# Silu on ScalarE in one instruction, in place of a tanh there and a product on VectorE

## The reference

```python
xz = xn @ W_in
xb, z = jnp.split(xz, 2, axis=-1)                 # 512 channels each
xp = jnp.pad(xb, ((0, 0), (1, 1), (0, 0)))
xb = conv_w[:, 0] * xp[:, :-2] + conv_w[:, 1] * xp[:, 1:-1] + conv_w[:, 2] * xp[:, 2:] + conv_b
xb = jax.nn.silu(xb)
dt = jax.nn.softplus(xb @ W_dt + b_dt)
Bi, Ci = xb @ W_B, xb @ W_C
# 16 states per channel, over the tokens:
#   h = exp(dt * A) * h + (dt * x) * B ;  y = sum over states of h * C
y = (y + D_param * xb) * jax.nn.silu(z)
return residual + y @ W_out
```

## Time and profile before

| | |
|---|---|
| median of 3 runs | 2777.06 us (2775.08 to 2786.98) |
| profiled execution | span 2779.7 us; its own time is told by this span alone |
| granted TensorE clock, mean | 0.941 |
| busy | PE 86%, DVE 87%, POOL 80%, ACT 56% of the span |
| table loads | 64 before L921, 49 before L1028 |

### The profile page before, as it was taken

How to read it: one execution, slowest core, us unless ns; L and a number is a source line. 1 busy time by engine, 2 the same in 40 slices (tenths; PEclk the granted TensorE clock), 3 DMA queues, 4 the chain that set the end, 5 groups by cost and what they waited for, 6 DMA issues and landing times.

```text
span 2779.7 us, 29004 instructions
## 1 busy us (share of the span) xinstructions
PE 2379.4 (86%) x9004; PEld 1687.3 (61%) x9004; DVE 2424.8 (87%) x2450; ACT 1565.3 (56%) x2961; POOL 2234.5 (80%) x1563
## 2 busy tenths in 40 slices
PE   3445798998989899898989999898999989898899
PEld 1222466666756666675666667666666756666678
DVE  2688999999999999999999999999999999999922
ACT  3556666566566656655665655566565556665311
POOL 1578888888888888888898888888888888987922
PEclk8677899999999899999999999999999999999999
DMA  4689898999989899998989989898998989898921
GB/s 113 172 209 231 220 236 219 229 237 218 239 221 235 218 227 235 222 236 214 234 224 238 232 220 244 213 233 218 241 231 218 241 205 235 222 245 210 241 64 50
DMA packets 338380, 596.80 MB, mean 215 GB/s; under 512 B 49696, under 2 KB 160288, under 8 KB 338224
## 3 DMA queue, kind: packets, MB, share of 16 engines
q0 software_dynamic: 72960, 243.30, 45.6%
q1 hardware_dynamic: 265264, 351.64, 40.3%
HBM read 349.89 MB, written 10.06 MB: 129 GB/s over the span
## 4 chain that ended last, share of the span: by engine, by line
PE 25%; POOL 22%; issue 17%; DVE 17%; ACT 10%; DMA 8%; SPq 0%; POOLq 0%; DVEq 0%; ACTq 0%
POOL unit L1199 9%; PE wbank L498 7%; DVE hbank L726 7%; DMA gsum<-unit 4%; POOL act L1166 4%; POOL gsum L1211 3%; PE mbank L510 3%; PE wbank L440 3%; DVE unit L740 3%; PE wbank L526 2%; PE wbank L388 2%; ACT z L849 2%; PE wbank L460 2%; DMA w_all<-w_scratch 2%; ACT hbank L1028 2%
## 5 line engine op out<-in xcount | busy, mean ns | idle before, releaser
L1199 POOL TENSOR_TENSOR unit<-dtx,b_bc 128x1024 f32<-128x1024 f32 x512 | 1345.9, 2639 | 10.8 <-DMA b_bc<-bc_scratch 8.9
L726 DVE TENSOR_TENSOR_SCAN hbank<-hbank,unit 128x1024 f32<-128x1024 f32 x512 | 1173.2, 2291 | 72.7 <-ACT hbank L1028 66.4
L1028 ACT ACTIVATE hbank<-dt,a_neg 128x512 f32<-128x512 f32 x1024 | 668.8, 681 | 303.6 <-DVE unit L740 269.6
L510 PE MATMUL mbank<-down_t,act 128*128 128x256 f32 x2048 | 525.6, 394 | 69.5 <-POOL act L1166 46.7
L740 DVE TENSOR_TENSOR unit<-hbank,c_bc 128x1024 f32<-128x1024 f32 x448 | 546.2, 1219 | 25.9 <-DVE hbank L726 1.8
L1166 POOL TENSOR_TENSOR act<-act,w_all 128x512 f32<-128x512 f32 x256 | 359.6, 1405 | 242.6 <-DVE act L704 222.9
L1211 POOL DMA_DIRECT2D gsum<-unit x448 | 444.0, 991 | 105.0 <-DMA gsum<-unit 50.8
L498 PE MATMUL wbank<-h_t,up_t 128*128 128x256 f32 x2048 | 503.6, 390 | 10.7 <-DVE gz L608 10.7
L510 PEld LDWEIGHTS mbank<-down_t,act 128*128 128x128 f32 x2048 | 397.5, 197 | 176.2 <-issue 64.8
L498 PE MATMUL wbank<-h_t,gate_t 128*128 128x256 f32 x2048 | 489.4, 382 | 13.4 <-DVE dt L600 11.4
L498 PEld LDWEIGHTS wbank<-h_t,up_t 128*128 128x128 f32 x2048 | 396.0, 195 | 108.8 <-DVE gz L608 29.2
(11 more groups left out here) (121 smaller groups left out, 2398.2 us busy)
## 6 DMA issues: line engine op xcount, KB each, us to landing
gsum<-unit POOLq DMA_DIRECT2D x448, 512.0 KB, 7.3
c_bc<-bc_scratch SPq DMA_DIRECT2D x464, 256.0 KB, 5.6
b_bc<-bc_scratch SPq DMA_DIRECT2D x448, 256.0 KB, 6.2
w_all<-w_scratch SPq DMA_DIRECT2D x256, 256.0 KB, 4.6
ht<-in_L_attn_x_dram SPq DMA_DIRECT2D x16, 512.0 KB, 6.0
w_out<-in_L_attn_W_out_dram SPq DMA_DIRECT2D x16, 512.0 KB, 6.2
ht<-in_L_attn_x_dram POOLq DMA_DIRECT2D x16, 512.0 KB, 8.4
out_dram<-xt SPq DMA_DIRECT2D x16, 512.0 KB, 3.3
```

What stands on the lines that cost most here:

```text
L510: m = eng.matmul(mbank[:, u * H:(u + 1) * H], act[:, (n - 1) % MOE_RING, j, u * P:(u + 1) * P], down_t[:, e, :], start=(e == 0 and u == 0) ...
L726: eng.tensor_tensor_scan(h, h, unit[:, g % RING, :, :].rearrange("p a t -> p (a t)"), 0.0, ALU.mult, ALU.add).then_inc(scanned, 1)
L1028: eng.activation(hbank[g % HB][:, a, :], dt[:, 2 * q + a, :], ACT.Exp, scale=a_neg[:, 2 * q + a, n:n + 1]).then_inc(decayed, 1)
L1199: eng.tensor_tensor(unit[:, g % RING, :, :], dtx[:, 2 * q:2 * q + 2, :], b_bc[:, s:s + 1, :].to_broadcast([P, 2, T]), ALU.mult).then_inc(d ...
```

## The change

ScalarE computes the silus whole, with its function Silu. `silu_inputs`: VectorE keeps the two taps and frees the bank with the second; ScalarE does one Silu of 128x1024 for two blocks, from both halves of `conv` into `xb`, behind the second block's taps. That Silu also waits, in the first pair, for the y product of the row before, a wait that VectorE had. `gates`: ScalarE does Silu of the bank into `gz`, in pairs where the second of each pair was, and frees the bank; VectorE's stage `gates` is gone. `mix` waits for the gate's `free`. The halvings go with it.

```diff
--- before.py
+++ after.py
...
@@ -255,8 +254,7 @@
 
         def xb_ready(need, row):
 
-            t = work.at["conv", row, DK - 1]
-            need.wait_ge(t.free, t.after)
+            need.wait_ge(silu_act, 2 * row + 2)
 
         def unit_freed(need, g):
 
@@ -523,7 +521,7 @@
                     eng.matmul(t.bank[:, :], diag_d[:, q, :], xb[:, xb_at(row, q), :], start=True, stop=False)
                     for k in range(2):
                         need.wait_ge(summed[k], 16 * LATER * (p + 1))
-                        m = eng.matmul(t.bank[:, :], half_ident[:, :], gsum[:, (2 * p + k) % SUMS, a, :], start=False,
+                        m = eng.matmul(t.bank[:, :], ident[:, :], gsum[:, (2 * p + k) % SUMS, a, :], start=False,
                                        stop=k == 1)
                     m.then_inc(t.full, 1)
                     yield
...
@@ -579,17 +577,11 @@
                     need.wait_ge(conv_act, n)
                     eng.scalar_tensor_tensor(out=cv[:, 1:T], in0=t.bank[:, 0:T - 1], scalar=conv_w[:, q, 0:1],
                                              in1=cv[:, 1:T], op0=ALU.mult, op1=ALU.add).then_inc(conv_v, 1)
-                    need.wait_ge(conv_v, 2 * n - 1)
+                    need.wait_ge(conv_v, n)
                     eng.scalar_tensor_tensor(out=cv[:, 0:T - 1], in0=t.bank[:, 1:T], scalar=conv_w[:, q, 2:3],
-                                             in1=cv[:, 0:T - 1], op0=ALU.mult, op1=ALU.add).then_inc(conv_v, 1)
-                    yield
-                    yield
-                    need.wait_ge(silu_act, n)
-                    if row and not pair:
-                        y = work.at["y", row - 1, q]
-                        need.wait_ge(y.full, y.after)
-                    eng.scalar_tensor_tensor(out=xb[:, xb_at(row, q), :], in0=t.bank[:, :], scalar=1.0, in1=cv, op0=ALU.add,
-                                             op1=ALU.mult).then_inc(t.free, 1)
+                                             in1=cv[:, 0:T - 1], op0=ALU.mult, op1=ALU.add).then_inc(t.free, 1)
+                    yield
+                    yield
                     yield
 
             def step_sizes(row, q):
@@ -598,15 +590,6 @@
                     yield
                     need.wait_ge(soft_act, 4 * (DK * row + m_ + 1))
                     eng.tensor_tensor(dt[:, m_, :], dt[:, m_, :], t.bank[:, :], ALU.add).then_inc(t.free, 1)
-                    yield
-                    yield
-
-            def gates(row):
-                for q in range(DK):
-                    t = work.at["gate", row, q]
-                    need.wait_ge(gate_act, DK * row + q + 1)
-                    eng.scalar_tensor_tensor(out=gz[:, q, :], in0=gz[:, q, :], scalar=1.0, in1=t.bank[:, :],
-                                             op0=ALU.add, op1=ALU.mult).then_inc(t.free, 1)
                     yield
                     yield
 
...
@@ -742,8 +725,9 @@
 
             def mix(row, pair):
                 for q in (2 * pair, 2 * pair + 1):
-                    t = work.at["y", row, q]
+                    t, z = work.at["y", row, q], work.at["gate", row, q]
                     need.wait_ge(t.full, t.after)
+                    need.wait_ge(z.free, z.after)
                     eng.tensor_tensor(gz[:, q, :], gz[:, q, :], t.bank[:, :], ALU.mult).then_inc(t.free, 1)
                     yield
                     yield
...
@@ -782,14 +766,11 @@
                 eng.scalar_tensor_tensor(out=row, in0=gsgn, scalar=-1.0, in1=gabs, op0=ALU.add,
                                          op1=ALU.mult).then_inc(mod_dve, 1)
             need.wait_ge(weights_in, 16 * N_LOADS)
-            eng.tensor_scalar(conv_w[:, :, :], conv_w[:, :, :], 0.5, None, ALU.mult).then_inc(scaled_w, 1)
-            eng.tensor_scalar(conv_b[:, :], conv_b[:, :], 0.5, None, ALU.mult).then_inc(scaled_w, 1)
             eng.tensor_scalar(choice_bias[:, :], choice_bias[:, :], 0.5, None, ALU.add).then_inc(scaled_w, 1)
             need.wait_ge(consts, 2)
             for m_ in range(DK):
-                eng.tensor_scalar(diag_d[:, m_, :], ident[:, :], d_par[:, m_:m_ + 1], 0.5, ALU.mult,
+                eng.tensor_scalar(diag_d[:, m_, :], ident[:, :], d_par[:, m_:m_ + 1], None,
                                   ALU.mult).then_inc(scaled_w, 1)
-            eng.tensor_scalar(half_ident[:, :], ident[:, :], 0.5, None, ALU.mult).then_inc(scaled_w, 1)
             need.wait_ge(a_exp, 1)
             eng.tensor_scalar(a_neg[:, :, :], a_neg[:, :, :], SLOWEST, -1.0, ALU.max, ALU.mult).then_inc(scaled_w, 1)
 
...
@@ -896,14 +877,19 @@
                     cv = conv[:, q % 2, :]
                     need.wait_ge(t.full, t.after)
                     if n > 2:
-                        before = work.at["conv", *divmod(n - 3, DK)]
-                        need.wait_ge(before.free, before.after)
+                        need.wait_ge(silu_act, (n - 1) // 2)
                     eng.activation(cv, t.bank[:, :], ACT.Identity, bias=conv_b[:, q:q + 1],
                                    scale=conv_w[:, q, 1:2]).then_inc(conv_act, 1)
                     yield
                     yield
-                    need.wait_ge(conv_v, 2 * n)
-                    eng.activation(t.bank[:, :], cv, ACT.Tanh).then_inc(silu_act, 1)
+                    if q % 2:
+                        for made in (work.at["conv", row, q - 1], t):
+                            need.wait_ge(made.free, made.after)
+                        if row and not pair:
+                            y = work.at["y", row - 1, q]
+                            need.wait_ge(y.full, y.after)
+                        x0 = xb_at(row, q - 1)
+                        eng.activation(xb[:, x0:x0 + 2, :], conv[:, :, :], ACT.Silu).then_inc(silu_act, 1)
                     yield
 
             def step_sizes(row, q):
@@ -936,13 +922,16 @@
                 yield
 
             def gates(row):
-                for q in range(DK):
-                    t = work.at["gate", row, q]
-                    need.wait_ge(t.full, t.after)
-                    if row:
-                        p = work.at["proj", row - 1, 1]
-                        need.wait_ge(p.full, p.after)
-                    eng.activation(gz[:, q, :], t.bank[:, :], ACT.Tanh, scale=0.5).then_inc(gate_act, 1)
+                for pair in range(2):
+                    yield
+                    yield
+                    for q in (2 * pair, 2 * pair + 1):
+                        t = work.at["gate", row, q]
+                        need.wait_ge(t.full, t.after)
+                        if row:
+                            p = work.at["proj", row - 1, 1]
+                            need.wait_ge(p.full, p.after)
+                        eng.activation(gz[:, q, :], t.bank[:, :], ACT.Silu).then_inc(t.free, 1)
                     yield
                     yield
 
...
```

More of the change, by code:

```diff
@@ L133, in build @@
         ident = sb("ident", [P, P])
-        half_ident = sb("half_ident", [P, P])
         conv_w = sb("conv_w", [P, DK, 3])
@@ L225, in build @@
         soft_act, dtx_made, dt_cut = sem("soft_act"), sem("dtx_made"), sem("dt_cut")
-        gate_act, bc_made, bc_out, w_made, w_stored = (
-            sem(n) for n in ("gate_act", "bc_made", "bc_out", "w_made", "w_stored"))
+        bc_made, bc_out, w_made, w_stored = (
+            sem(n) for n in ("bc_made", "bc_out", "w_made", "w_stored"))
         b_in, c_in = [sem(f"b{k}_in") for k in range(B_RING)], [sem(f"c{k}_in") for k in range(C_RING)]
@@ L544, in _ @@
             need.wait_ge(weights_in, 16 * N_LOADS)
-            need.wait_ge(scaled_w, 9)
+            need.wait_ge(scaled_w, 6)
             stage_of = {"turn_in": turn_in, "silu_first": lambda r: silu_inputs(r, 0),
@@ L799, in _ @@
             stage_of = {"silu_first": lambda r: silu_inputs(r, 0),
-                        "silu_last": lambda r: silu_inputs(r, 1), "gates": gates,
+                        "silu_last": lambda r: silu_inputs(r, 1),
                         "step_sizes0": lambda r: step_sizes(r, 0), "step_sizes1": lambda r: step_sizes(r, 1),
```

## The result

The changed kernel takes 2813.24 us (median of four runs, 2812.25 to 2819.44) against 2780.24 of the kernel before (four runs): a ratio of 1.0123, 95% interval 1.0101 to 1.0145. The span of its profiled execution is 2812.4 us, 32.7 over the 2779.7 of before. The forecast was 19.8 over.

The account below looks back on a forecast made before the run. VectorE was taken as nearest its bound, three engines being over 85% busy. Per row 0.5 + 2.25 - 0.84 - 0.4 = +1.5 us, 22.5 in 15 rows, less 2.7 before the loop: 2797 us, range 2785 to 2815.

Parts of the forecast that it names:

- VectorE's saving: Products into xb and gz leave VectorE: 8 x 0.60 = 4.8 us per row, 77 us in 16 rows.
- Eight loads a row: Four Silu groups per row on ScalarE, decays between them: 8 table loads of 1.283 us, 10.3 us per row.
- I let it run ahead: At the inputs, the table load before xb's Silu runs ahead of that Silu's waits; 1.28 us more per pair otherwise.
- rival 4: Loads stand behind the waits at the inputs: 38 us more than forecast, 2835 us; chance 0.08.
- load back until 1151.5, experts' tanh until 1152.1: First input pair: a load back precedes the experts' tanh, so VectorE's expert product begins 1.75 us later.
- rival 3: Silu shares a set with Tanh, not Exp; input load back comes behind experts' tanh: 2774 us, no change; chance 0.22.
- +2.25 us: Delay per row over both input pairs, as VectorE's expert product waits for the experts' tanh behind Silu and load back.
- +0.5 us at the gates: Cost per row of the gates' Silus and loads, estimated between 0 and +1.4; VectorE's 2.4 us saved there buys nothing.
- this wait takes up 0.84, and small gaps on GpSimd about 0.4: After the inputs, VectorE's later tanh wait and GpSimd gaps absorb 0.84 and 0.4 us of each row's delay.
- -2.7 us before the loop: Row 0's inputs: ScalarE's identity of one block runs beside VectorE's taps of the other, products dropped, saving 2.7 us.

Follow-up runs that it names:

- later Silu: Changed kernel with each input pair's Silu moved behind the experts' tanh on ScalarE: 2754.02 us with a one-element Silu ahead of the waits, 2755.33 us without it.
- early load: Changed kernel plus a one-element Silu ahead of each input pair's waits, so the table load runs in them: 2774.12 us, 0.9973 of the kernel before.
- the kernel with the inputs alone: Changed kernel with the gates put back as before (tanh on ScalarE, product on VectorE), only the inputs changed: 2811.05 us, 1.0104 of the kernel before.
- without loads: Changed kernel with Tanh written for every Silu, so silus are not computed and the 126 added loads go: 2765.63 us, 0.9947 of the kernel before.

## Why the prediction came out as it did

The direction, the place and the kind of wait were right: loads on ScalarE, VectorE held at the inputs by the experts' tanh behind the Silu, nothing to gain at the gates. The size was too small, +19.8 us for +32.7. Two steps failed in the sum: the 1.24 us a row that later waits and gaps were to take up, and the saving before the loop, which put the loads of row 0 at nothing. By its steps:

- **VectorE's saving.** Foreseen 77 us, 71.6 less busy. Its worth, 2.4 us a row at the inputs and none at the gates, is what the kernel with the later Silu shows (2.33).
- **Eight loads a row.** Right: 126 against 128; the Silus of row 0 share loads. 1283 ns each, and no drain beside them: at 1164.24 the Silu starts 0.02 us after its load ended. The drain of about 1380 ns that the Trainium skill ("ScalarE: Activation LUTs", What ACT_TABLE_LOAD costs) adds to a switch is not seen here either.
- **"I let it run ahead".** Wrong. The load stands behind the waits (88.3 us of idle before 31 loads), as rival 4 had it. The row of before that I leaned on the earlier trace rows had a single wait. That a load with one wait ran ahead doesn't say where it stands among three.
- **"load back until 1151.5, experts' tanh until 1152.1".** Wrong too, the other way: Tanh is in Silu's set (rival 3), so no load is between them. In the changed kernel the tanh starts at 1165.20, when the Silu is about to end, and the load of the way back comes before the decays. The two errors are of 1.28 us each and nearly cancelled: +2.25 us foreseen for the inputs, +1.9 measured. The early load takes the load out from behind the waits and leaves no load ahead of the tanh, which is the scene of rival 3, and it measured what that rival said, about no change: 2774, 0.3% under before. So the term's size was right by luck, and the experiments, not the total, showed that.
- **+0.5 us at the gates.** Measured +0.2 in the median for the changed kernel against before, 0.5 (118.1 against 117.6) against the kernel with the inputs alone; by the scatter of that column, anything from nothing to 0.5. That the gates' banks come free at about the same times was wrong: TensorE's wait before L496's matmuls of `up_t`, which was 10.7 us in all, is 57.1, and 29.1 of it is for the gates' Silus. The scan behind the gates was foreseen 1.4 us late and is 2.0 late, counted from the copy; at the scan behind the norm it is back at 0.0, as the wait of 1.94 us takes it up. Here a later wait does take up a delay.
- **"this wait takes up 0.84, and small gaps on GpSimd about 0.4".** Wrong, and the larger of the two steps that failed in the sum: 15 x 1.24 = 18.6 us. The wait at 1196.64 is 0.83 us, where it was 0.84. The column to the next copy is 22.3 us in all ten kernels. The tanh it waits for stands behind the step sizes on ScalarE, whose matmuls wait for a bank that VectorE frees (below, TensorE waits 0.89 us for VectorE's product); so the late VectorE makes that tanh just as late. With the later Silu VectorE comes 2.33 us early to this place, and there too the tanh comes early with it: the wait is 1.12 us, only 0.3 longer, and the column is the same. A wait takes up a delay only if what it waits for doesn't hang on the delayed engine. The rows of TensorE's and of ScalarE's timeline (in the kernel before these matmuls show no wait for VectorE, but they start the same 8.8 us behind its product with the tanh of the second pair):

```profile
1187.21 3.70 PE L398 MATMUL wbank<-xb,w_dt 128*128 128x512 f32 x8 [0.89 <-DVE act L680]
```

```profile
1190.95 0.69 ACT L902 ACTIVATE dt<-wbank,b_dt 128x512 f32<-128x512 f32 x1 [0.31 <-PE wbank L398]
...
1196.01 0.60 ACT L1007 ACTIVATE etanh<-wbank 128x512 f32<-128x512 f32 x1
```

- **-2.7 us before the loop.** Wrong, by 4: the first scan starts at 97.59, before at 96.08. The sum had no load here, and two stand in the path: one ahead of the first pair's Silu, behind its waits, and one at 83.20, since the first Exp of the step sizes now needs a load of its own. From VectorE's first tap to its first scan it is 35.39 us before, 36.25 in the changed kernel and 33.42 without loads. So the new pairs would have given 2.0 us, and the loads cost 2.8. That it isn't 2.7 has its reason in the pairs, which don't run beside each other as I had it: the next block's identity needs both halves of conv, free only when the Silu is done. Another 0.65 us lies ahead of the first tap (61.34 against 60.69); over the ten kernels that start scatters from 60.09 to 62.20, and I put it down to nothing.

```profile
65.73 1.28 ACT L892 ACT_TABLE_LOAD   x1 [1.64 <-DVE z L581]
...
83.20 1.28 ACT L905 ACT_TABLE_LOAD   x1
84.50 0.58 ACT L905 ACTIVATE wbank<-wbank 128x512 f32<-128x512 f32 x1
85.09 1.28 ACT L907 ACT_TABLE_LOAD   x1
86.39 0.58 ACT L907 ACTIVATE wbank<-wbank 128x512 f32<-128x512 f32 x1
```

With nothing absorbed and these measured terms the working gives 15 x 1.9 + 1.5 = 30 us, or 33 with the 0.2 of the gates, for 32.7 measured. It has no term for the 1.65 us behind the last copy, which come in the last row's steps and which I haven't followed, so the last 2 or 3 us of the agreement are not shown.

## What to carry to other kernels

Before a function of another table set goes into an in-order queue, look at what stands behind it that another engine waits for, not at the engine's free share (44% of ScalarE was free, and two loads a row cost 1.4%, early load against changed); put the urgent work ahead of the switch (2755 us), or, where that can't be, the switch into a wait (2774); both together gave no more than the first (2754). Work taken from the busiest engine pays only where the row's chain passes: of eight products a row four paid, and these only once the tanh was out of the way. When a delay is said to be taken up by a later wait, follow that wait's releaser back: if it hangs on the engine that is late, nothing is taken up.

## What the runs showed of the hardware

A table load ran ahead of the wait of its activation where there was one (in both kernels the first load of all, at 0.79 us with 9.45 us of waiting behind it in the changed kernel, and the load before row 0's first decay), and behind them where there were several (31 of 31 at the inputs). A switch cost its 1283 ns: in the changed kernel, where no wait stands beside a load, the gap to its neighbours is about 0.02 us. No load stood between a Silu of the inputs and the experts' tanh behind it (28 times), and one always stood between a Silu and the next Exp: Silu's set as loaded here has Tanh in it and not Exp. A Silu of 128x1024 from SBUF to SBUF took 1057 ns, one of one element per partition 203 ns. That the place of the load follows from the number of waits, rather than from the semaphores' kinds, wasn't tried.
